# First cross attention of a transformer kernel: weight division and V copies on ScalarE, copies on GpSimd behind the normalised keys, negated scores, another order on VectorE

## The reference, cut to what matters

```
xn = layernorm(ctx);  ln = layernorm(latents)
q  = ln @ Wq.T
kv = concat([xn @ Wkv.T, ln @ Wlkv.T])          # 257 + 32 = 289 rows
k, v = split(kv)
qn = rmsnorm(q, qn_g) * 64 ** -0.5
kn = rmsnorm(k, kn_g)                            # k / sqrt(mean(k*k)) * kn_g, per head
attn = where(mask, qn @ kn.T, -3.4e38)
out  = softmax(attn) @ v
return out @ Wo.T + bo
```

## Time and profile before

| | us |
|---|---|
| median of 3 runs | 3326.92 |
| lowest and highest | 3326.33 to 3331.58 |
| the profiled execution | 3332.58 |
| its span, first to last instruction | 3330.8 |

### The profile page before, as it was taken

How to read it: one execution, slowest core, us unless ns; L and a number is a source line. 1 busy time by engine, 2 the same in 40 slices (tenths; PEclk the granted TensorE clock), 3 DMA queues, 4 the chain that set the end, 5 groups by cost and what they waited for, 6 DMA issues and landing times. The chain is left out here.

```text
span 3330.8 us, 64318 instructions
## 1 busy us (share of the span) xinstructions
PE 2791.1 (84%) x21884; PEld 2167.8 (65%) x21885; DVE 2207.0 (66%) x5353; ACT 1457.6 (44%) x3947; POOL 696.1 (21%) x808
## 2 busy tenths in 40 slices
PE   6688888799978999999997899995846777769993
PEld 3466666466666888988896577774323333469993
DVE  6588888566527777777774577776548999842222
ACT  3433333255504444444442477772257667103331
POOL 3355655122100000000000122221022222012224
PEclk8899999899978999999999999997969999969997
DMA  3121221000030000000000011110200000261112
GB/s 90 49 56 53 57 57 40 33 1 0 1 158 2 1 1 1 0 0 0 0 1 16 22 31 31 31 32 31 107 0 1 1 1 1 101 248 34 36 36 89
DMA packets 69108, 120.71 MB, mean 36 GB/s; under 512 B 10192, under 2 KB 51504, under 8 KB 64368
## 3 DMA queue, kind: packets, MB, share of 16 engines
q1 hardware_dynamic: 65568, 109.76, 10.0%
q0 software_dynamic: 3408, 9.31, 1.0%
HBM read 99.19 MB, written 17.69 MB: 35 GB/s over the span
## 5 line engine op out<-in xcount | busy, mean ns | idle before, releaser
L1259 PE MATMUL s_ps<-s3e_col_hot,s3e_row_hot 128*128 128x64 f32 x2048 | 249.9, 276 | 29.2 <-DVE s3e_col_hot L1439 28.5
L1259 PEld LDWEIGHTS s_ps<-s3e_col_hot,s3e_row_hot 128*128 128x128 f32 x2048 | 243.5, 194 | 44.8 <-issue 27.9
L1284 PE MATMUL s_ps<-s_up,s3e_gh 128*128 128x256 f32 x1024 | 258.5, 398 | 7.3 <-DVE s3e_gh L1447 7.3
L1295 PEld LDWEIGHTS s_ps<-s3e_xT,s_down 128*128 128x128 f32 x2048 | 250.3, 194 | 7.4 <-issue 1.0
L1295 PE MATMUL s_ps<-s3e_xT,s_down 128*128 128x128 f32 x2048 | 251.2, 277 | 0.0
L1337 ACT ACTIVATE s3e_gh<-s_ps 128x512 f32<-128x512 f32 x128 | 76.3, 597 | 380.6 <-PE s_ps L1295 380.4
L1284 PEld LDWEIGHTS s_ps<-s_up,s3e_gh 128*128 128x128 f32 x1024 | 191.9, 197 | 33.8 <-DVE s3e_gh L1447 10.6
L1447 DVE TENSOR_TENSOR s3e_gh<-s_ps,s3e_gh 128x512 f32<-128x512 f32 x128 | 88.3, 690 | 188.1 <-PE s_ps L1259 188.1
L1688 ACT ACTIVATE s4b_pr<-s4b_sc,s4b_nm 128x257 f32<-128x257 f32 x256 | 127.8, 503 | 108.9 <-DVE s4b_nm L1736 108.8
L191 POOL MEMSET s4q_half<- 128x1 f32 x1 | 0.1, 99 | 820.5 <-POOLq L2686 820.5
L2591 ACT ACTIVATE s6e_hT<-s_ps,s_b 128x128 f32<-128x128 f32 x312 | 84.9, 383 | 187.2 <-PE s_ps L2564 187.2
(11 more groups left out here) (428 smaller groups left out, 6709.1 us busy)
## 6 DMA issues: line engine op xcount, KB each, us to landing
s_w<-p_w SPq DMA_DIRECT2D x16, 1024.0 KB, 13.4
s4b_cT<-ctxT SPq DMA_DIRECT2D x64, 192.8 KB, 2.4
s1b_cx<-ctx SPq DMA_DIRECT2D x64, 192.0 KB, 2.7
s1b_cT<-ctxT SPq DMA_DIRECT2D x64, 192.0 KB, 2.9
s_results<-s6e_y SPq DMA_DIRECT2D x39, 128.0 KB, 1.7
s_down<-p_down SPq DMA_DIRECT2D x1, 4096.0 KB, 21.7
s_up<-p_up SPq DMA_DIRECT2D x1, 4096.0 KB, 31.0
s_silu_z<-s5p_sz SPq DMA_DIRECT2D x4, 1024.0 KB, 4.5
```

What stands on the lines that cost most here:

```text
L1259: mm = pe.matmul(banks[:, G_BANK + i % 2, j * M:(j + 1) * M], lhsT=row_hot[:, i % 2, j, :], rhs=col_hot[:, i % 2, j, :], start=True, stop= ...
L1284: mm = pe.matmul(banks[:, Y_BANK, 0:D], lhsT=gh[:, o.u, e, :], rhs=up[:, e, :], start=e == 0, stop=e == NE - 1)
L1295: mm = pe.matmul(banks[:, H_BANK + i % 2, tok(e)], lhsT=down[:, k, i * CH + e, :], rhs=xT[:, c.u, k, :], start=k == 0, stop=k == KT - 1)
```

## The change

Six edits, all in `phase1_attention`.

- VectorE no longer multiplies `pr` by `ri`. It only makes the reciprocal, and ScalarE multiplies, in place, behind the two copies into `kT` and ahead of the squares.
- The copy of `v3` moves from GpSimd to ScalarE, behind the exponential.
- GpSimd's `qb` and `kT` copies wait in addition for `kn_ready`, the normalised keys of the same batch.
- The scores are made with the opposite sign, so that one minimum gives `nm` and the negation falls away; the exponential takes scale -1.
- The addition of epsilon moves from VectorE to GpSimd, ahead of the power for `crs`. The factor 1/64 of the mean goes into the squares. Three links, waits of VectorE on its own last instruction, fall away with these edits.
- VectorE makes `vv` at the end of its step, behind the sums of the squares, where it stood ahead of the keys of the next batch.

```diff
@@ gpsimd
+                    pool.wait_ge(kn_ready, c.b + 1)
                     pool.tensor_tensor(qb[:, c.u, :, :].rearrange("p k (h q) -> p k h q", h=H), ...
                     pool.tensor_tensor(kT[:, c.u, :, 2 * P:NK], KE[:, :, c.b, :], ...
-                c = item(LAG_AT)
-                if c:
-                    after(pool, pv, c.b - 1)
-                    pool.tensor_tensor(v3[0:S + 1, c.u, :], V3[:, c.b, :], bc(one[0:S + 1, :], S + 1, D), ALU.mult).then_inc(v3_ready, 1)
                 c = item(LAG_TR)
                 if c:
+                    pool.wait_ge(cmv_ready, c.b + 1)
+                    after(pool, crs_ready, c.b)
+                    pool.tensor_tensor(cve[:, c.u, :], cmv[:, c.u, :, 1], bc(eps[:], P, 2), ALU.add).then_inc(cve_ready, 1)
                     pool.wait_ge(cve_ready, c.b + 1)
                     after(pool, vv_ready, c.b - 1)
                     pool.tensor_tensor(crs[:, c.u, :], cve[:, c.u, :], bc(half[:], P, 2), ALU.pow).then_inc(crs_ready, 1)
@@ scalar
-                    act.activation(pr[:, a.u, :], sc[:, a.u, :], ACT.Exp, bias=nm[:, a.u, :], accum_out=rs[:, a.u, :]).then_inc(pr_ready, 1)
+                    act.activation(pr[:, a.u, :], sc[:, a.u, :], ACT.Exp, bias=nm[:, a.u, :], scale=-1.0, accum_out=rs[:, a.u, :]).then_inc(pr_ready, 1)
+                    after(act, pv, a.b - 1)
+                    act.activation(v3[0:S + 1, a.u, :], V3[:, a.b, :], ACT.Copy).then_inc(v3_ready, 1)
@@ scalar, behind the copies into kT
+                if a:
+                    act.wait_ge(ri_ready, a.b + 1)
+                    act.activation(pr[:, a.u, :], pr[:, a.u, :], ACT.Copy, scale=ri[:, a.u, :]).then_inc(share_ready, 1)
                 if c:
                     act.wait_ge(kr_ready, c.b + 1)
-                    act.activation(sq[:, c.u, :, :], kn[:, c.u, :, :], ACT.Square).then_inc(sq_ready, 1)
+                    act.activation(sq[:, c.u, :, :], kn[:, c.u, :, :], ACT.Square, scale=HD ** -0.5).then_inc(sq_ready, 1)
@@ vector
-                    link(dve.scalar_tensor_tensor(sc[:, a.u, :], dropped[:, a.b, :], -BIG, banks[:, S_BANK, 0:NK], ALU.mult, ALU.add))
-                    link(dve.tensor_reduce(mx[:, a.u, :], sc[:, a.u, :], AXX, ALU.max))
-                    dve.tensor_scalar(nm[:, a.u, :], mx[:, a.u, :], -1.0, None, ALU.mult).then_inc(sc_ready, 1)
+                    link(dve.scalar_tensor_tensor(sc[:, a.u, :], dropped[:, a.b, :], BIG, banks[:, S_BANK, 0:NK], ALU.mult, ALU.subtract))
+                    dve.tensor_reduce(nm[:, a.u, :], sc[:, a.u, :], AXX, ALU.min).then_inc(sc_ready, 1)
@@ vector, behind the keys' normalisation
                     dve.wait_ge(pr_ready, a.b + 1)
-                    link(dve.reciprocal(ri[:, a.u, :], rs[:, a.u, :]))
-                    dve.tensor_scalar(pr[:, a.u, :], pr[:, a.u, :], ri[:, a.u, :], None, ALU.mult).then_inc(share_ready, 1)
-                if n:
-                    dve.wait_ge(values, n.b + 1)
-                    if o:
-                        dve.wait_ge(pv, o.b + 1)
-                    scaled(vv, V_BANK, n, slice(D, 2 * D)).then_inc(vv_ready, 1)
+                    dve.reciprocal(ri[:, a.u, :], rs[:, a.u, :]).then_inc(ri_ready, 1)
@@ vector, at the end of the step
-                    link(ins)
-                    dve.tensor_scalar(cve[:, t.u, :], cmv[:, t.u, :, 1], LN_EPS, None, ALU.add).then_inc(cve_ready, 1)
+                    ins.then_inc(cmv_ready, 1)
                 if c:
                     dve.wait_ge(sq_ready, c.b + 1)
                     link(dve.tensor_reduce(ss[:, c.u, :], sq[:, c.u, :, :].rearrange("p j (h d) -> p (j h) d", h=H), AXX, ALU.add))
-                    dve.tensor_scalar(ss[:, c.u, :], ss[:, c.u, :], 1.0 / HD, 1e-16, ALU.mult, ALU.max).then_inc(ss_ready, 1)
-            skewed(dve, B, 3, step, link, 6)
+                    dve.tensor_scalar(ss[:, c.u, :], ss[:, c.u, :], 1e-16, None, ALU.max).then_inc(ss_ready, 1)
+                if n:
+                    dve.wait_ge(values, n.b + 1)
+                    if o:
+                        dve.wait_ge(pv, o.b + 1)
+                    scaled(vv, V_BANK, n, slice(D, 2 * D)).then_inc(vv_ready, 1)
+            skewed(dve, B, 3, step, link, 3)
```

More of the change, by code:

```diff
@@ L579, in phase1_attention @@
         sc = sb("sc", [P, U, NK])
-        mx, nm = sb("mx", [P, U, 1]), sb("nm", [P, U, 1])
+        nm = sb("nm", [P, U, 1])
         pr = sb("pr", [P, U, NK])
         v3 = sb("v3", [P, U, D])
+        eps = sb("eps", [P, 1])
         rs, ri = sb("rs", [P, U, 1]), sb("ri", [P, U, 1])
         pT = sb("pT", [P, U, 3, P])
-        (cve_ready, crs_ready, kr_ready, keys, values, sq_ready, vv_ready, ss_ready, rn_ready, kn_ready,
-         k_tr, kT_ready, ke_ready, qb_ready, zeroed, scores, sc_ready, pr_ready, share_ready, p_tr, pT_ready, pv, oT_ready, v3_ready,
+        (cmv_ready, cve_ready, pr_ready, crs_ready, kr_ready, keys, values, sq_ready, vv_ready, ss_ready, rn_ready, kn_ready,
+         k_tr, kT_ready, ke_ready, qb_ready, zeroed, scores, sc_ready, ri_ready, share_ready, p_tr, pT_ready, pv, oT_ready, v3_ready,
          one_ready, dve_link) = s.sems(
-            "cve_ready crs_ready kr_ready keys values sq_ready vv_ready ss_ready rn_ready kn_ready "
-            "k_tr kT_ready ke_ready qb_ready zeroed scores sc_ready pr_ready share_ready p_tr pT_ready pv oT_ready v3_ready "
+            "cmv_ready cve_ready pr_ready crs_ready kr_ready keys values sq_ready vv_ready ss_ready rn_ready kn_ready "
+            "k_tr kT_ready ke_ready qb_ready zeroed scores sc_ready ri_ready share_ready p_tr pT_ready pv oT_ready v3_ready "
             "one_ready dve_link")
@@ L600, in step @@
                 c = item(0)
-                after(sp, cve_ready, c.b - 1)
+                after(sp, cmv_ready, c.b - 1)
                 sp.dma_start(cx[:, c.u, :, :], I["ctx_768"][c.b, 0:2 * P, :].rearrange("(j p) c -> p j c", p=P)).then_inc(cx_loaded[c.u], 16)
@@ L611, in _ @@
             pool.memset(one[:], 1.0).then_inc(one_ready, 1)
-            pool.wait_ge(one_ready, 1)
+            pool.memset(eps[:], LN_EPS).then_inc(one_ready, 1)
+            pool.wait_ge(one_ready, 2)
             pool.wait_ge(zeroed, 2)
@@ L694, in _ @@
         def _(act):
-            act.wait_ge(zeroed, 1)
+            act.wait_ge(zeroed, 2)
             def step(item):
```

## The result

The changed kernel takes 3334.14 us (median of 20 runs, 3331.36 to 3342.47), the kernel before 3329.47 (20 runs on the same chips, 3326.02 to 3334.89). The ratio is 1.0017, with a 95% interval from 1.001 to 1.0024: slower by 0.17%, or 4.7 us. The forecast was slower by 17.7 us. They did not go in the loop that the sum is about. (The forecast stood on a median of 3 runs of the kernel before, 3326.92; with 20 runs it is 2.55 us higher, and the text compares differences.)

The account below looks back on a forecast made before the run. VectorE's queue bounded the kernel before; afterwards a dependence loop through ScalarE, VectorE and GpSimd takes 7.39 us a step against 7.10. 61 x 0.29 = 17.7 us more makes 3344.6 us from 3326.92, range 3330 to 3358.

Parts of the forecast that it names:

- 1: copies into `kT` start: TensorE transposes the keys; ScalarE starts its first copy into `kT` 0.75 us after the keys' multiplication ends.
- 2: the division starts: ScalarE's two copies into `kT` take 0.84 us, less 0.09 overlap: 0.75, sum 1.50.
- 3: the squares start: ScalarE's new multiplication of `pr` takes 0.52 us, less overlap 0.43, ahead of the squares: sum 1.93.
- 4: the squares end; the sum is scaled: ScalarE's squares take 0.63 us, sum 2.56; VectorE sums them and scales the sum: 3.31.
- 5: `vv` ends: `vv`, now last in VectorE's step, starts 0.12 us after the scaling and takes 0.86: sum 4.29.
- 6: `crs` ends, less overlap: GpSimd's power `crs` waits for `vv`: handover 0.08 us, power 0.70, less 0.04 overlap: sum 5.03.
- 7: the next keys start: GpSimd's `rn`, queued behind `crs`, takes 1.64 us, then 0.03 to VectorE: sum 6.70.
- 8: one turn: VectorE's keys' multiplication takes 0.69 us, closing the loop at 7.39 a step, where before it was 7.10.
- The division and the keys cost less: Rival for steps 3 and 8: prices 0.37 and 0.55 us, step 7.10, no change, 3327; chance 0.13.
- Faster: Rival: ScalarE is not in the loop; step 6.55 us, 34 us less, 3293; chance 0.08.
- the lock: VectorE with two SBUF inputs and GpSimd reading SBUF exclude each other; holding copies gains 0.40 us a step, 3301.
- Slower still: Rival: ScalarE's handovers lose their overlap and the division takes 0.60 us; step 7.65, 3361; chance 0.03.

Follow-up runs that it names:

- the queue of `crs` ahead of `rn`: Changed kernel, on GpSimd the power for `rn` put ahead of `crs`: 3251.76 us; or with `vv` back in its old place on VectorE: 3255.95 us.
- ScalarE's part: Changed kernel with ScalarE's squares put ahead of the division of the weights: 3310.76 us, ratio 0.9934.
- the held copies: Kernel before, with only GpSimd's copies waiting for the normalised keys and the V copy moved to ScalarE: 3278.86 us, ratio 0.9847.
- the groups: The ten kernels in two groups of five by the place of VectorE's code (1182 or 1184 rows ahead; 1152 or 1280): `retrieve` takes 747.8 and 732.1 us.
- the two padded kernels: Unread VectorE memsets added behind the attention: 28 in the changed kernel, 3345.31 us; 96 in the kernel before, 3317.34 us.
- the paused one: Kernel before with 16 GpSimd memsets (some 17 us) between the attention loop and the projection: 3350.05 us, ratio 1.0055.
- `rn` first: Changed kernel with GpSimd's power for `rn` put ahead of the epsilon addition and the power for `crs`: 3251.76 us, ratio 0.976.

## Why the prediction was wrong, point by point

**The sum for the loop was right.** By its own steps, with time 0 at the end of the keys' multiplication (351.20 + 0.69 = 351.89 in the timeline of after):

| step | forecast, us | measured, us |
|---|---|---|
| 1: copies into `kT` start | 0.75 | 352.64: 0.75 |
| 2: the division starts | 1.50 | 353.37: 1.48 |
| 3: the squares start | 1.93 | 353.80: 1.91 |
| 4: the squares end; the sum is scaled | 2.56; 3.31 | 354.42: 2.53; 355.17 is the scaling's start, 3.28 |
| 5: `vv` ends | 4.29 | 355.25 + 0.88: 4.24 |
| 6: `crs` ends, less overlap | 5.03 | 356.94: 5.05 |
| 7: the next keys start | 6.70 | 358.61: 6.72 |
| 8: one turn | 7.39 | 359.30: 7.41 |

The mean step is 7.38. The two prices that no row of before showed came out as taken: the division 0.533 us (0.52), the keys' multiplication 0.692 (0.69). Two small values off the forecast cancel: `vv` follows the scaling after 0.08 us and not 0.12, and GpSimd takes `vv` over after 0.15 and not 0.08. VectorE's wait for `rn` is 1.63 us (1.5 forecast), for the squares 0.90 (0.8), TensorE's for the keys 1.12 (1.2). Attention ends 16.8 us later, where the sum for the whole loop says 17.7. Each turn of its argument has its own run: the queue of `crs` ahead of `rn` (opened, it is worth 1.3 us a step), ScalarE's part (0.40), the held copies (0.40 by the multiplication alone).

**The step that failed** is the one that makes a step's price the kernel's: the 17.7 us for the loop were added to the time of the whole ("The profiled execution, 3332.58 us, would come to 3350.3"), with the other phases put at no change, as phases "whose instructions the change leaves as they are". It leaves the instructions and not their place. A term was missing: 14 to 17 us off for the four loop turns of `retrieve` whose stall disappears, and about 3.6 us on for the 28 turns of the second attention whose loop overhead grows. With the means of the groups, 16.8 - 12.5 is 4.3 us, to be held against 4.7 by the medians. With the two traces alone, 16.8 - 17.3 + 3.1 is 2.6; the rest of the table, -4.3 and +2.0, lies in stretches for which I found no cause (the one ahead of `retrieve` is 425.5, 421.2, 423.4, 424.3 and 425.4 us in before, after, the two padded kernels and the paused one, in no order of the two groups).

The row was there to be read before: four times 2.4 us by "issue" on VectorE in `retrieve`, with TensorE waiting about 2.5 us behind three of them and a granted clock of 0.72 after the first. I looked at the rest of the program only for what the change edits. What I could not have had from it is the sign or the size for this change: the trace of before shows that the loop's head stalls, but not at which place in the program it would stop doing so.

**The rivals.** "The division and the keys cost less" gave 3327 and is nearest in time but wrong in mechanism: neither was cheaper. "Faster" needed the squares by 1.75 us; their sum could only start at 2.56 (354.45). Its price for the lock, 0.40 us a step, is what the held copies alone gave the multiplication, but the loop of `vv` took it. (By the prediction's own 61 intervals that price gives 3302.5, where it says 3301.) "Slower still" would have needed lost overlaps; ScalarE's starts kept theirs (353.37 is 0.11 ahead of the end of the copies at 353.48).

**The rule on multiplications.** The prediction weighed the Trainium skill's advice, "ScalarE: Activation LUTs", section "Rules for kernel authors", to multiply on VectorE, at 0.43 us a step. It costs 0.40 where the division stands ahead of the squares. With `rn` first the division is still on ScalarE, ahead of the squares, and TensorE is busy for 335.00 of 335.00 us, so the division can cost little or nothing there; no run moved it in that kernel.

**What stays open.** Whether other places exist that are better still for both loops (two good ones were seen: in both, the rows ahead of the loop are a whole multiple of 128, 1152 and 1280, which may be chance, since no other place near them was tried). Why the stall comes at one place and not at the other: that it comes with fetches is shown, which rule of the place decides is not. Also why the second attention's overhead moves by 0.13 us a turn, for which I have the row and not a mechanism; and what varies by a few us in the stretches named above.

## What to carry to other kernels

A change that moves an engine's instruction count moves all later code of that engine, and a hardware loop far behind it can win or lose a stall at its head: before forecasting a small difference, look for waits by "issue" at loop heads everywhere in the program, and give the difference that much room (here 14 to 17 us in one stage and 8 to 12.5 in all, nearly as much as the loop's own change). To learn what an edit is worth, compare at landmarks by stage, or fill the program to its old length. And work taken off the busiest engine is worth only what the longest loop of dependences lets through: the same edits give -2.4% with `rn` ahead of `crs` and +0.2% with it behind. Both figures contain what the place gave, about 0.4% (12.5 of 3331 us, an estimate from the table).

## What the runs showed of the hardware that I had not expected

- 96 useless VectorE instructions made the kernel 13.6 us faster (ratio 0.9961), by ending a stall of 2.4 us in four turns of a later loop.
- Such a stall can cost TensorE more than its length. At one turn it was idle for 2.50 us, and then 8 matmuls took 3.58 us in place of 1.95, with the granted clock at 0.72 over 6 us; four turns cost 16.7 us, where VectorE stood for 9.5.
- The head of one and the same loop, that of the second attention, cost VectorE 6.3 us in 28 turns or 9.9, by the place of its code alone (0.22 or 0.35 us a turn).
